# Two edits to a graph-and-expert kernel: sums over all nodes in 25 parts, and gathered rows turned by DMA

## The reference, cut to what matters

```python
def _spmm(h, src, dst, inv_deg):            # mean over the edges that end in a node
    agg = jax.ops.segment_sum(h[src], dst, num_segments=h.shape[0])
    return agg * inv_deg[:, None]

# graph part, on layernorm(x)
x = silu(h @ W_in.T + b_in)
out = term = x
for i in range(1, 7):                       # K_STEPS = 6, gamma = 0
    term = _spmm(term, src, dst, inv_deg) / i
    out = out + term
x1 = x_input + out @ W_out.T + b_out

# expert part, on layernorm(x1), layer-normed again with gamma and beta to xn
logits = xn @ Wr + br                       # 8 experts
top_vals, top_idx = top_k(logits, 2); w = softmax(top_vals)
y = sum over the two experts e:  w_e * (gelu(xn @ W1[e] + b1[e]) @ W2[e] + b2[e])
result = x1 + y
```

## Time and profile before

| | |
|---|---|
| median of 3 runs | 1383.98 us (1383.05 to 1384.16) |
| the profiled execution's own time | 1385.32 us |
| its span, first to last instruction | 1383.5 us |
| PE busy | 1192.7 us, 86% |
| VectorE busy | 728.0 us, 53% |
| ScalarE busy | 368.1 us, 27% |
| GpSimd busy | 158.1 us, 11% |
| mean granted TensorE clock | 0.929 |

### The profile page before, as it was taken

The page is one execution under the profiler, slowest core; times in us unless marked ns, Lnnn a source line. Parts: engine busy times, 40 slices in busy tenths (PEclk is TensorE's granted clock), DMA queues, the critical chain, the costliest instruction groups (busy, mean ns, idle before and its releaser), DMA issues.

```text
span 1383.5 us, 27811 instructions
## 1 busy us (share of the span) xinstructions
PE 1192.7 (86%) x7796; PEld 826.7 (60%) x7796; DVE 728.0 (53%) x1480; ACT 368.1 (27%) x722; POOL 158.1 (11%) x171
## 2 busy tenths in 40 slices
PE   4895999999999999999369999988999359999870
PEld 2784776665666666666146666655666338777750
DVE  7588999963443343431135344324554755555545
ACT  1574655540000000010012111101211224344333
POOL 2000000000000000000000000000111224565540
PEclk8897999999999999999679999999999559999995
DMA  6110010023211112147753233211433111222229
GB/s 156 31 53 19 24 39 30 30 56 97 62 49 59 53 53 69 41 153 142 81 127 110 69 97 103 72 29 57 122 112 106 49 31 56 77 68 70 71 62 255
DMA packets 74762, 105.04 MB, mean 76 GB/s; under 512 B 11939, under 2 KB 60891, under 8 KB 74491
## 3 DMA queue, kind: packets, MB, share of 16 engines
q1 hardware_dynamic: 62500, 72.44, 18.2%
q0 software_dynamic: 9824, 24.61, 7.7%
q10 hardware_dynamic: 2356, 6.93, 2.0%
HBM read 76.99 MB, written 37.49 MB: 83 GB/s over the span
## 4 chain that ended last, share of the span: by engine, by line
PE 66%; DMA 10%; issue 9%; DVE 8%; ACT 2%; POOL 2%; DVEq 1%; another core or an unknown queue 1%; SPq 1%; ACTq 1%; POOLq 0%
PE ps L1647 35%; PE ps L1625 7%; PE ps L1777 5%; PE ps L1693 4%; PE ps L1761 4%; PE ps L1593 4%; DMA w_dram<-v_a 3%; DVE v_b L1059 3%; DMA v_a<-L_ffn_W 2%; DMA adj<-y_dram 2%; PE ps L1561 2%; PE ps L1572 1%; DMA v_b<-xs_dram,v_a 1%; DMA h_ring<-h_dram 1%
## 5 line engine op out<-in xcount | busy, mean ns | idle before, releaser
L1647 PE MATMUL ps<-v_b,adj 125*125 125x512 f16 x1250 | 275.7, 384 | 37.0 <-DVE t_hi L1066 35.0
L1647 PE MATMUL ps<-v_a,adj 125*125 125x512 f16 x1375 | 297.3, 379 | 0.0
L1647 PEld LDWEIGHTS ps<-v_b,adj 125*125 x1250 | 172.8, 138 | 139.7 <-issue 43.0
L1647 PEld LDWEIGHTS ps<-v_a,adj 125*125 (+1 forms) x1375 | 187.6, 137 | 108.9
L1059 DVE TENSOR_TENSOR v_b<-v_b 125x2560 f16<-125x2560 f16 x125 | 180.2, 1485 | 7.1 <-PE ps L1593 6.5
L1066 DVE SCALAR_TENSOR_TENSOR t_hi<-ps,cinv,t_hi 125x256 f32<-125x256 f32 x125 | 60.2, 482 | 222.2 <-ACT t_hi L820 222.2
L820 ACT ACTIVATE t_hi<-ps,cinv 125x256 f32<-125x256 f32 x125 | 59.0, 472 | 421.9 <-PE ps L1647 383.6
L1693 PE MATMUL ps<-v_b,adj 125*125 125x512 f16 x625 | 143.4, 389 | 5.1 <-DVEq L1234 3.3
L797 ACT ACTIVATE adj<-ps 125x625 f32 (+1 forms) x125 | 111.8, 906 | 75.2 <-PE ps L1593 74.4
L1625 PE MATMUL ps<-v_a,adj 125*125 125x512 f16 x500 | 123.4, 380 | 0.0
L1761 PE MATMUL ps<-v_b,adj 128*128 128x128 f16 x1344 | 116.9, 222 | 6.5 <-issue 5.1
(11 more groups left out here) (235 smaller groups left out, 914.9 us busy)
## 6 DMA issues: line engine op xcount, KB each, us to landing
h_ring<-h_dram SPq DMA_DIRECT2D x125, 125.0 KB
v_a<-L_ffn_W SPq DMA_DIRECT2D x32, 256.0 KB, 3.5
v_b<-L_ffn_W SPq DMA_DIRECT2D x32, 256.0 KB, 3.2
adj<-w_dram SPq DMA_DIRECT2D x16, 512.0 KB, 4.8
w_dram<-w_hi SPq DMA_DIRECT2D x32, 128.0 KB, 1.9
hx_dram<-h_dram POOLq DMA_DIRECT2D x1, 3125.0 KB, 13.0
hx_dram<-x POOLq DMA_DIRECT2D x1, 3125.0 KB, 20.3
hx_dram<-L_gnn_b_out POOLq DMA_DIRECT2D x1, 3125.0 KB, 63.6
```

What stands on the lines that cost most here:

```text
L1647: last = te.matmul(ps[0:NP, u, :], of_tile(adj[0:NP, 0:ADJ], i, u, a * NP, NP), source[:, a, :], start=(a == 0), stop=(a == T - 1))
```

## The change

The three transfers of the sums leave their place behind the all-reduce. A function `sums(n, done)` makes the same three for the n-th of HX = 25 parts of 125 rows, and GpSimd runs it 25 times ahead of its wait for `w_top_ok`; part n waits until `tile_ps` is at 26 + 2n. SyncE waits for the full count of `hx_ok` at the same place as before. The slow branch for graphs that the windows don't cover, not taken with these inputs, makes the sums again.

In the expert stage `transposed` is empty on PE and VectorE. SyncE, after its last store of rows, issues for each tile a transposing DMA transfer from `x_g` to `xT16`, once the gather has landed and `hidden` of the tile four before has ended. GpSimd's gather, and `hidden` on PE, wait for that transfer's semaphore `xT_in`. `result` waits for its own inputs by name (`hs_ok`, `y_ok`), where it waited for a VectorE copy that came later in VectorE's order.

```diff
--- before.py
+++ after.py
@@ -52,6 +52,9 @@
     EARLY_AT = 2
     XR = 4
     LAG = 3
+    HX = 25
+    HX_EVERY = 2
+    assert N % HX == 0 and T + 1 + HX * HX_EVERY <= 3 * T + 1
     assert FT % FU == 0
 
 
@@ -341,7 +344,7 @@
             ve_ok sd_ok z_ok xn2_ok xnT_ps xnT_ok lg_ps lg_ok xhi_ok xs_ok piece_used piece_hi w16_out
             b2_in w_in w_top_ok w_all_ok b1_top_ok b1_all_ok wsc_ok hx_ok ex_in ex_ok cnt_in cnt_ok rt_const rt_by_c rt_done tables_ok tok_ps idx_ok
             pool_turn cover_sum cover_ps cover_ok term_ok e_const e_in e_col e_oh e_mm e_acc e_read e_term e_rows
-            xg_T xgT_ok ffn_h gelu_ok hs_ok ffn_y y_ok y2_ok comb_ok""".split()
+            ffn_h gelu_ok hs_ok ffn_y y_ok y2_ok comb_ok""".split()
         S = {n: sem(n) for n in names}
         h_in = [sem(f"h_in{r}") for r in range(2)]
         h_out = [sem(f"h_out{r}") for r in range(3)]
@@ -350,6 +353,7 @@
         xs_out = [sem(f"xs_out{r}") for r in range(WIN)]
         piece_in = [sem(f"piece_in{r}") for r in range(2)]
         g_in = [sem(f"g_in{r}") for r in range(FU)]
+        xT_in = [sem(f"xT_in{r}") for r in range(XR)]
         y_out = [sem(f"y_out{r}") for r in range(FR)]
         yc_in = [[sem(f"y{k}_in{i}") for i in range(NB)] for k in range(TOP)]
         out_sem = sem("out_sem")
@@ -555,7 +559,7 @@
 
             sp.wait_ge(S["term_ok"], 1)
 
-            sp.wait_ge(S["hx_ok"], 48)
+            sp.wait_ge(S["hx_ok"], 48 * HX)
 
             def bc(v, n):
                 return bass.AP(v.tensor, 0, [[0, 128], [1, n]])
@@ -598,6 +602,11 @@
             for w in range(T - 6, T):
                 rows_out(w, w % WIN)
 
+            for j in range(FT):
+                sp.wait_ge(g_in[j % FU], 16 * (j // FU + 1))
+                need(sp, S["ffn_h"], j - XR + 1)
+                sp.dma_start_transpose(xT16[j % XR], x_g[j % FU]).then_inc(xT_in[j % XR], 16)
+
             for r in range(FR):
                 sp.wait_ge(y_out[r], 16 * (FT // FR))
             for i in range(NB):
@@ -629,6 +638,23 @@
                 g.indirect_dma_start(g_edges[:, r, :, :].rearrange("p s k -> p (s k)"), None, edge_rows,
                                      bass.IndirectOffsetOnAxis(ap=start_row[0:NP, r:r + 1], axis=0),
                                      ).then_inc(S["gathered"], 16)
+
+            def sums(n, done):
+
+                part = slice(n * N // HX, (n + 1) * N // HX)
+                rows = N // HX
+                g.dma_start(hx_dram[part, :], h_dram[part, :]).then_inc(S["hx_ok"], 16)
+                pool.wait_ge(S["hx_ok"], done + 16)
+                g.dma_start(hx_dram[part, :], x[part, :], max_dma_last_dim=8192, accum_op=ALU.add).then_inc(S["hx_ok"], 16)
+                pool.wait_ge(S["hx_ok"], done + 32)
+                g.dma_start(hx_dram[part, :], bass.AP(b_out.tensor, 0, [[0, rows], [1, D]]), accum_op=ALU.add).then_inc(S["hx_ok"], 16)
+                pool.wait_ge(S["hx_ok"], done + 48)
+
+            for slot in range(3):
+                pool.wait_ge(h_out[slot], H_OUT[slot])
+            for n in range(HX):
+                pool.wait_ge(S["tile_ps"], T + 1 + n * HX_EVERY)
+                sums(n, 48 * n)
 
             pool.wait_ge(S["w_top_ok"], 1)
             g.partition_all_reduce(w_all, w_top, 128, bass.bass_isa.ReduceOp.max).then_inc(S["w_all_ok"], 1)
@@ -674,14 +700,9 @@
                 pool.wait_ge(S["e_rows"], 16 * (STEPS + 1))
                 g.dma_start(h_v, term_e).then_inc(S["e_rows"], 16)
                 pool.wait_ge(S["e_rows"], 16 * (STEPS + 2))
-
-            for slot in range(3):
-                pool.wait_ge(h_out[slot], H_OUT[slot])
-            g.dma_start(hx_dram, h_dram).then_inc(S["hx_ok"], 16)
-            pool.wait_ge(S["hx_ok"], 16)
-            g.dma_start(hx_dram, x, max_dma_last_dim=8192, accum_op=ALU.add).then_inc(S["hx_ok"], 16)
-            pool.wait_ge(S["hx_ok"], 32)
-            g.dma_start(hx_dram, bass.AP(b_out.tensor, 0, [[0, N], [1, D]]), accum_op=ALU.add).then_inc(S["hx_ok"], 16)
+                for n in range(HX):
+                    sums(n, 48 * (HX + n))
+                pool.wait_ge(S["hx_ok"], 96 * HX)
 
             pool.wait_ge(S["term_ok"], 1)
             g.memset(ident2, 0.0)
@@ -727,7 +748,7 @@
             def gather(j):
                 u = j % FU
                 if j >= FU:
-                    pool.wait_ge(S["xg_T"], j - FU + 1)
+                    pool.wait_ge(xT_in[(j - FU) % XR], 16 * ((j - FU) // XR + 1))
                 g.indirect_dma_start(x_g[u], None, xs_dram,
                                      bass.IndirectOffsetOnAxis(ap=idx_g[:, j:j + 1], axis=0)).then_inc(g_in[u], 16)
 
@@ -1486,11 +1507,7 @@
             dve.wait_ge(S["b2_in"], 16 * NE)
 
             def transposed(j):
-                u, r = j % FU, j % 2
-                dve.wait_ge(S["xg_T"], j + 1)
-
-                need(dve, S["ffn_h"], j - XR + 1)
-                v.tensor_copy(xT16[u % XR], ps[:, r, :].bitcast(F16)[:, 0:2 * D].rearrange("k (b s) -> k b s", b=2 * DK)).then_inc(S["xgT_ok"], 1)
+                pass
 
             def hidden(j, b, e, part):
                 u, r = j % FU, j % 2
@@ -1738,22 +1755,13 @@
             pe.wait_ge(S["w_in"], 16 * 2 * NE)
 
             def transposed(j):
-                u, r = j % FU, j % 2
-                pe.wait_ge(g_in[u], 16 * (j // FU + 1))
-                if 2 <= j < 2 + LAG:
-
-                    pe.wait_ge(S["xgT_ok"], j - 1)
-                for b in range(2 * DK):
-                    last = te.transpose(ps[:, r, :].bitcast(F16)[:, b * 128:(b + 1) * 128], x_g[u][:, b * 128:(b + 1) * 128], ident16)
-                last.then_inc(S["xg_T"], 1)
+                pass
 
             def hidden(j, b, home):
                 u, r = j % FU, j % 2
                 if b == 0:
 
-                    if j < LAG:
-                        pe.wait_ge(S["xgT_ok"], j + 1)
-
+                    pe.wait_ge(xT_in[j % XR], 16 * (j // XR + 1))
                     need(pe, S["gelu_ok"], j - 1)
                 for n, (low, part) in enumerate(((0, 0), (0, 1), (1, 0))):
                     for k in range(DK):
@@ -1766,13 +1774,9 @@
 
             def result(j, b, part, alone):
                 u, r = j % FU, j % 2
-                if b == 0 and alone:
+                if b == 0:
                     pe.wait_ge(S["hs_ok"], j + 1)
-                    pe.wait_ge(S["y_ok"], j - 1)
-                elif b == 0:
-
-
-                    pe.wait_ge(S["xgT_ok"], j + LAG + 1)
+                    need(pe, S["y_ok"], j - 1)
                 for n, (hp, low) in enumerate(((h_hi, 0), (h_hi, 1), (h_lo, 0))):
                     last = te.matmul(ps[:, 4 + r, 0:D], hp[u % FR][:, b, :],
                                      w_block(part, 1, low, b * D, D),
```

## The result

| | before | after |
|---|---|---|
| median | 1384.07 us (1383.05 to 1384.78, 4 runs) | 1350.24 us (1348.30 to 1352.38, 4 runs) |
| profiled span | 1383.5 us | 1348.7 us |
| mean clock | 0.929 | 0.943 |

What follows compares the result with a forecast made beforehand. PE's matmuls were taken as the bound, except in diffusion step 3, which lost 40.5 us behind GpSimd's large transfers. 1385.3 - 40.5 - 12.3 + 1 = 1333.5, so 1332 for the median; range 1324 to 1400.

Steps and rivals of the forecast that it cites:

- part 1: Third diffusion step: sums in 25 parts replace three whole-array GpSimd transfers; -40.5 us, bounds 0 and -40.5.
- A group: Diffusion, GpSimd: three awaited 125 KB transfers after every second tile; 11.3 us, bounds 9.0 and 12.9, free up to 11.6.
- C: Start of the third diffusion step: sums lag at 12.9 us a group, PE waits 33 us; 1365 us; chance 0.08.
- D: Third diffusion step: weight pieces cause the hole, so splitting the sums does nothing; 1372 us; chance 0.03.
- The start: Expert stage: the first hidden matmul waits for gather and transpose; +1 us, bounds 0 and +3.
- The transposing transfer: Expert stage, SyncE: 56 transfers of 128 KB, 2 to 3 us a tile, hidden behind PE's 3.4.
- T: Expert stage: time per tile of the transposing transfer, taken as 2 to 3 us.
- A: Expert stage, SyncE's queue: transposing transfers without overlap set the pace; at 5.6 us each +110, 1454 us; chance 0.22.
- B: Expert stage: transposing transfers share engines with gathers and scatters, T 3.7 to 4.3 us; 1347 to 1381; chance 0.09.
- Part 2's gain: Expert stage: DMA transposes remove 224 PE transposes, 0.22 us a tile on the chain; -12.3 us, bounds 0 to -20.

Runs made afterwards that it cites:

- sums alone: Only the sums in 25 parts, transposes left on PE and VectorE, against the kernel before: 1322.82 us (0.9718) on the first chip, 1323.90 (0.9724) on the third.
- the transfers beside: 56 transposing transfers that nobody reads, added to the kernel with only the sums in 25 parts: 1330.77 us, 0.9776 of the kernel before, third chip.

## Why the prediction was right or wrong

The direction and most of the size came from part 1. That the time fell inside the range of 1324 to 1400 is in part luck: its upper end was left open for a slow transfer, and the loss that filled it had another cause.

**Part 1, right.** The term was -40.5 and measured -40.6, for the reason given: step 3 became a step 4. A group was put at 11.3 us and took 11.35, against a limit of 11.6; the forecast called 11.3 too high since it counts the data twice, and there it erred: the groups fell behind, the all-reduce came at 620.3 against a limit of 625, so C's stall was only 0.25 us a group away. The parts landed after 2.5, 3.3 and 4.1 us, so the estimate of 2.3 us each was low for the accumulating ones. D is out: sums alone give 38.0 and 35.4 us on two chips, by the medians 2.6 and 5.2 less than step 3 gave here; that rest is not traced.

**The start, right.** First gather to first hidden matmul was 5.9 us and is 6.4: +0.5 against +1.

**The transposing transfer, right, with room.** T was taken as 2 to 3 us a tile and is 1.30 overlapped. A loses from 3.63 on and B began at 3.7, and even in line it is 2.8, so neither happened. The Trainium skill's figure for a transpose by DMA ("VectorE: DVE Perf Modes", The three transpose paths) made an estimate of 5.2 us a tile; the runs contradict that estimate for this shape, with 2.8 us in line and 1.30 in a row. The Trainium skill also says ("Advanced Engine Details and Errata", X-Bar Transpose) that such transfers are as fast as plain ones. By landing time this case agrees: 2.4 us alone, where plain transfers of 128 KB of this kernel land after 1.9 to 4.0 us. No run has a plain transfer within SBUF beside it, and the issue is dearer, 1.19 us against 0.27 to 0.7 for SyncE's plain ones.

**Part 2's gain, wrong: this is the step that failed.** "Removed from PE: 224 transposes, 0.22 us per tile on the chain, 56 x 0.22 = 12.3 us", value -12.3, bounds 0 to -20. Measured on one chip it is +10.5 us (1334.4 against 1323.9), outside the bounds, and alone +11.3; in the first measurement the stretch of the hidden matmuls grew by 3.2. Two things were missing. First, the transposes lay on the chain, but beneath them PE's sequencer did the next tile's register load and addresses; the forecast read "some 0.25 us of issue" in the earlier trace rows as a constant next to them and not as the part of that work that still stuck out. Putting transposes back costs 1.3 us, taking the load away gains 12.5, moving it moves the gap, and on the third chip the time from the first hidden block to the next result block grows by 0.21 us where the transposes took 0.22. Second, transfers that are hidden are not free: 56 beside an unchanged stage cost 6.9 us in the medians (4.9 in the stage), with later gathers and more issue gaps. The forecast asked only whether T fits in the period (B and A), never what a T that fits does to the gathers. The account on the third chip: 10.5 + 12.3 = 22.8 us went missing. 6.9 of it are the transfers beside, some 11 the cover, and about 5 are left, for which the longer time at the tile's end and the spread of single profiles are candidates, not shown.

**Chip to chip.** The forecast was made on a trace in which the stage takes 3.63 us a tile, and the kernel with the sums alone takes 3.24 and 3.29 on the faster chips. On the slower one PE's stream has gaps that wait for nothing shown, before and after the change alike; they are not explained here. The sums alone were not run on a chip of that kind, so what part 2 costs there by medians is not known; both edits have the ratios 0.9756 and 0.9732 there and 0.9805 on a faster one.

The best version is the sums alone: 1323.9 us against 1334.4 for both and 1359.3 before, on one chip.

## What to carry to other kernels

A large transfer without haste, put in small pieces into steps whose DMA engines are little used, gave back the whole stall here, but add up the series of waits and compare it with the last moment at which what is queued behind it may run. Before small work is removed from an engine that bounds the stage, look at what its sequencer does under it: address arithmetic and register loads that the removed work covered come out bare. Three tests show it: put idle work back, move the load, and compare the time between the blocks behind the removed work. A transfer that fits in the period can still delay the gathers around it: price it by adding it without its use.

## What was not expected of the hardware

- A transposing transfer of 128 x 512 f16 within SBUF: 1.19 us of SyncE to issue, 544 packets, landing after 2.4 us alone (two of 32 took 7.3 and 10.3), 1.30 us each when overlapped. At the start of the stage the first one's user starts 3.4 us after its issue.
- GpSimd's transfers of 125 KB from DRAM to DRAM land in 2.5 us as a copy, 3.3 us accumulating, and 4.1 us accumulating from one repeated row of 1 KB.
- Both edits with no register load in PE's stream (constant place) run in stretches with a granted clock of 0.90 to 0.96 and gaps up to 1.3 us; the sums alone with the same constant keep 1.00, with gaps by issue up to 1.1 us. Why they differ is open.
- A PE register load from SBUF takes 0.30 us (56 of them, 0.306 in the median) and an address instruction 32 ns, 23 of these a tile.
- One kernel's time differs by 27 us between chips (before: 1359.3 and 1386.1). For both edits the profiled spans differ by 18.7 us between the third chip and the second, and 16.2 of them are the expert stage (202.6 and 218.8 us).
